# Two shared banks and a narrow layer norm in the windowed-attention layers, a later start for the weight loads, and a respaced state-space stage

## The reference, cut to what matters

```python
q, k = l2norm(q) * qs, l2norm(k) * ksc     # 16 heads of 64, then rotary tables on q and k
sim = jnp.einsum('bhwie,bhwje->bhwij', bq, bk2) * QK_SCALE
attn = jax.nn.softmax(jnp.where(mask, -jnp.finfo(sim.dtype).max, sim), -1)   # window 32
out = jnp.einsum('bhwij,bhwje->bhwie', attn, bv2)
...
def ffn_layer(x, g, bln, W1, b1, W2, b2):
    mu = x.mean(-1, keepdims=True)
    var = ((x - mu) ** 2).mean(-1, keepdims=True)
    xn = (x - mu) / jnp.sqrt(var + 1e-05) * g + bln
    hg = xn @ W1 + b1
    a, gate = jnp.split(hg, 2, -1)
    return a * jax.nn.gelu(gate, approximate=False) @ W2 + b2
for i in range(6):
    x = attn_layer(shift_tokens(x), ...) + x
    x = ffn_layer(shift_tokens(x), ...) + x
```

## Time and profile before

| | us |
|---|---|
| median of 3 runs | 6522.08 (6519.73 to 6525.92) |
| the profiled execution | 6522.74, its span 6520.8 |
| PE busy over the span | 5878.9 (90%) |
| DVE busy | 4384.8 (67%) |
| ACT busy | 3402.6 (52%) |
| POOL busy | 2289.2 (35%) |
| windowed attention, from its first projection (3236.6) to the end | 3284 |
| state-space stage, from its first measure (1791) to its last gather (2478) | about 690 |

### The profile page before, as it was taken

One profiled execution on the slowest core, in us unless ns is written; L12 is line 12 of the kernel. 1 busy time (PEld: TensorE's weight loads), 2 busy tenths in 40 slices (PEclk: granted clock), 3 DMA queues, 4 the chain that ended last, 5 costly groups with the idle time before them and its releaser, 6 DMA issues.

```text
span 6520.8 us, 129965 instructions
## 1 busy us (share of the span) xinstructions
PE 5878.9 (90%) x51681; PEld 3219.8 (49%) x51681; DVE 4384.8 (67%) x7178; ACT 3402.6 (52%) x5560; POOL 2289.2 (35%) x1597
## 2 busy tenths in 40 slices
PE   7999878999677778998689999999999999999998
PEld 3555554444422225765445555555555555555554
DVE  4656434454288894334678888888878788887885
ACT  3444324656144443444456656666666666665664
POOL 0111101222034441000055555555555555555553
PEclk9999978999688888998799999999999999999998
DMA  5555302333100000000011111111111111111110
GB/s 138 115 115 119 89 0 53 80 82 83 44 3 0 0 0 1 1 0 1 24 36 32 40 43 34 31 47 37 34 45 38 33 44 40 34 39 41 38 37 24
DMA packets 298945, 275.95 MB, mean 42 GB/s; under 512 B 40580, under 2 KB 289572, under 8 KB 298148
## 3 DMA queue, kind: packets, MB, share of 16 engines
q1 hardware_dynamic: 298372, 268.00, 17.7%
HBM read 30.88 MB, written 2.10 MB: 5 GB/s over the span
## 4 chain that ended last, share of the span: by engine, by line
PE 33%; issue 5%; DVE 5%; POOL 5%; ACT 2%; DMA 0%; POOLq 0%; DVEq 0%; SPq 0%; ACTq 0%
PE banks L2254 7%; PE banks L2289 6%; PE banks L2324 5%; PE banks L2309 4%; PE banks L2267 3%; PE banks L2341 3%; DVE local_probs L2559 2%; POOL local_rot L2653 2%; POOL local_ssum L2645 2%; PE banks L2363 2%; PE banks L2313 2%; PE banks L2274 1%; ACT local_probs L2455 1%; DVE local_gate L2584 1%; DVE local_sin L2540 1%
## 5 line engine op out<-in xcount | busy, mean ns | idle before, releaser
L2645 POOL TENSOR_TENSOR local_ssum<-local_sq 128x512 f32<-128x512 f32 x384 | 697.5, 1816 | 2145.1 <-ACT local_sq L2433 2144.6
L2653 POOL TENSOR_TENSOR local_rot<-local_rot,local_inv_all 128x512 f32<-128x512 f32 x768 | 964.6, 1288 | 94.1 <-DMA local_inv_all<-local_inv 93.6
L2254 PE MATMUL banks<-local_y,local_Wqkv 128*128 128x512 f32 x1536 | 823.0, 618 | 64.0 <-ACT local_sq L2433 61.2
L2559 DVE TENSOR_TENSOR local_probs<-banks,band 128x576 f32<-128x576 f32 x768 | 546.2, 753 | 185.4 <-PE banks L2289 180.1
L2455 ACT ACTIVATE local_probs<-local_probs,local_npeak 128x1152 f32<-128x1152 f32 x384 | 482.8, 1257 | 357.1 <-DVE local_probs L2559 357.1
L2539 DVE TENSOR_TENSOR local_rot<-banks,local_rotary_scaled 128x512 f32<-128x512 f32 x768 | 525.6, 684 | 191.1 <-PE banks L2254 185.6
L2433 ACT ACTIVATE local_sq<-banks 128x512 f32<-128x512 f32 x768 | 459.4, 598 | 253.6 <-DVE local_sin L2540 244.8
L2546 DVE TENSOR_TENSOR local_rot<-local_rot,local_sin 128x1024 f32<-128x1024 f32 x384 | 513.7, 1338 | 41.9 <-DVE local_sin L2540 2.3
L2449 ACT COPY local_v<-banks 128x512 f32<-128x512 f32 x384 | 224.9, 586 | 594.1 <-PE banks L2267 593.6
L2289 PEld LDWEIGHTS banks<-local_rot 32*128 32x128 f32 x12288 | 416.7, 186 | 225.0 <-issue 200.8
L2540 DVE TENSOR_TENSOR local_sin<-banks,local_rotary_scaled 128x512 f32<-128x512 f32 x768 | 522.4, 680 | 0.0
(11 more groups left out here) (400 smaller groups left out, 10561.4 us busy)
## 6 DMA issues: line engine op xcount, KB each, us to landing
local_inv_all<-local_inv SPq DMA_DIRECT2D x768, 128.0 KB, 2.7
favor_half_norm_all<-favor_half_norm SPq DMA_DIRECT2D x512, 128.0 KB, 3.0
cosine_inv_all<-cosine_inv SPq DMA_DIRECT2D x256, 128.0 KB, 2.6
favor_rden<-favor_inv SPq DMA_DIRECT2D x256, 64.0 KB, 2.1
cosine_rden<-cosine_inv_den SPq DMA_DIRECT2D x256, 64.0 KB, 2.1
local_Wqkv<-in_L_ffn_Wqkv_quads SPq DMA_DIRECT2D x36, 256.0 KB, 2.9
local_Wo<-in_L_ffn_Wo_quads SPq DMA_DIRECT2D x6, 512.0 KB, 4.1
experts_w_W<-in_L_ffn_W SPq DMA_DIRECT2D x1, 2048.0 KB
```

The lines of the kernel that those rows point to most:

```text
L2254: pe.matmul(seqs(banks[:, QK_BANK, :]), Wqkv[:, at:at + P], y_group(g), start=True, stop=True).then_inc(qk_projected, 1)
L2559: dve.tensor_tensor(probs[:, e % 3, r:r + 2, :], banks[:, S_BANK + r:S_BANK + r + 2, 0:SCORES], consts["band"].unsqueeze(1).broadcast_to([ ...
L2645: pool.tensor_tensor(ssum[:, n % 2, m, :], sq[:, 0, :], sq[:, 1, :], ALU.add).then_inc(square_summed, 1)
L2653: pool.tensor_tensor(a, a, twice(inv_all[:, n % 2, m, of_seq(s)]), ALU.mult).then_inc(united, 1)
```

## The change

- The start: only four constants, the weights of favor and x are loaded ahead of favor; the other five constants and the weights of router, cosine, int4, mamba and hgrn are issued by SP between favor's own transfers, in its steps 1 to 5.
- State space: measure, normalize, turn and copy of the next group stand four steps earlier (steps 12 to 15 of the group before); the output projection is cut in halves in steps 3 and 4, and the addition comes in step 5.
- Windowed attention, banks: P0 and P2 use bank 0, P1 and P3 bank 1, which they share with V0 and V1. The denominators go to bank 0, ahead of the values. `take_den` is cut in two: its Ln (`log_den`) stands ahead of the exponential of the probabilities, its Exp (`invert_den`) where the whole stood.
- PE's order: `score` of the even sequence stands ahead of `project_v(2i)` and `norm`. DVE masks ahead of the clamp, ACT squares ahead of the copy of v.
- The MLP's norm: means (step 4G+7) and variances (4G+8) are taken by 4 matmuls of 128 columns, each into 32 partitions, one per quarter of the tokens; ACT works on 128x128 instead of 128x512, and SP spreads each quarter back over 128 partitions by 4 transfers. POOL subtracts the mean (in place of the centering matrix and DVE's copy); `scale_mlp` stands behind `sum_squares(2i)`, no longer ahead of it.
- Ahead of the loop only group 0 is normed; groups 1 to 7 are measured, normed and turned in steps 0 to 7. The rotary tables are made in two halves, one of them at the end of the layer before.

```diff
+                    if i == LOADS:
+                        for tile, source in w["later_consts"]:
+                            sp.dma_start(tile, source).then_inc(w["consts_loaded"][0], 16)
+                    if 0 < i - LOADS <= len(w["later"]):
+                        w["later"][i - LOADS - 1].load(sp)
+                sp.wait_ge(*w["consts_loaded"])
...
-        0, 1, 2, 3, 5, 7, 8, 9, 10, 11, 12, 13, 14
-    GATE, WAY_OUT, ADD_OUT = 2, 3, 4
-    FIRST, LAST = -NS, N + ADD_OUT
+        -4, -3, -2, -1, 5, 7, 8, 9, 10, 11, 12, 13, 14
...
-    QK_BANK, V_BANK, S_BANK, O_BANK, X_BANK = 0, 1, 2, 6, 7
+    DEN_BANK, V_BANK, S_BANK, O_BANK, X_BANK = 0, 1, 2, 6, 7
+    qk_bank = lambda c: (DEN_BANK, V_BANK)[c % 2]
...
-                    if c:
-                        pe.wait_ge(squared, c)
+                    if half:
+                        pe.wait_ge(v_copied, c // 2 + 1)
+                    elif n >= 3:
+                        pe.wait_ge(den_logged, 2 * n - 5 + m)
+                    elif c:
+                        pe.wait_ge(squared, c - 1)
...
-                    if j >= 6:
-                        pe.wait_ge(den_logged, j - 5)
-                    elif j:
-                        pe.wait_ge(v_copied, j)
+                    if j:
+                        pe.wait_ge(squared, 2 * j)
...
+                    at_step = n + 2 + s
                     pe.wait_ge(exped, e + 1)
+                    if at_step < N:
+                        pe.wait_ge(squared, 4 * at_step + 3 - 2 * s)
+                    elif e:
+                        pe.wait_ge(den_logged, e)
+                    for lo, hi, tile in ((0, BAND, 0), (BAND, SCORES, 1)):
+                        for r in range(4):
+                            at = tile * P
+                            last = pe.matmul(banks[32 * r:32 * r + 32, DEN_BANK, at:at + hi - lo], consts["ones"][:, 0:32],
+                                             probs[:, e % 3, r, lo:hi], start=(tile == 0), stop=(tile == 1), skip_group_check=True)
+                    last.then_inc(den_summed, 1)
...
-                def center_mlp(G):
-                    take_x(centered, G + 1)
+                def mean(G):
+                    take_x(mean_taken, G + 1)
                     pe.wait_ge(added, 2 * G + 2)
-                    pe.matmul(seqs(banks[:, X_BANK, :]), center[:], y_group(G % GROUPS), start=True, stop=True).then_inc(centering, 1)
+                    for c in range(GT):
+                        at = c % ST * P
+                        last = pe.matmul(banks[32 * c:32 * c + 32, X_BANK, 0:P], consts["ones"][:, 0:32],
+                                         y[:, 2 * (G % GROUPS) + c // ST, at:at + P], start=True, stop=True)
+                    last.then_inc(y_summed, 1)
 
                 def variance(G):
                     take_x(var_logged, G + 1)
                     pe.wait_ge(mlp_squared, G + 1)
-                    pe.matmul(banks[:, X_BANK, :], consts["ones"], msq[:], start=True, stop=True).then_inc(var_summed, 1)
+                    for c in range(GT):
+                        last = pe.matmul(banks[32 * c:32 * c + 32, X_BANK, 0:P], consts["ones"][:, 0:32], msq[:, c * P:(c + 1) * P],
+                                         start=True, stop=True)
+                    last.then_inc(var_summed, 1)
...
                 for i in range(LAST + 1):
                     if i < N:
                         project(4 * i)
+                    if (e := within(2 * (i - 2))) is not None:
+                        score(e)
+                    if (G := mlp_at(i, 7)) is not None:
+                        mean(G)
+                    if i < N:
                         project_v(2 * i)
                     if 1 <= i <= N:
                         norm(i - 1)
-                    if (e := within(2 * (i - 2))) is not None:
-                        score(e)
...
-                def take_den(e):
-                    act.wait_ge(valued, e + 1)
+                def log_den(e):
+                    act.wait_ge(den_summed, e + 1)
                     if e >= 2:
                         act.wait_ge(normalized, e - 1)
-                    act.activation(rden[:, e % 2, :], banks[:, V_BANK, 0:SEQ], ACT.Ln, scale=UP).then_inc(den_logged, 1)
+                    act.activation(rden[:, e % 2, :], banks[:, DEN_BANK, 0:SEQ], ACT.Ln, scale=UP).then_inc(den_logged, 1)
+
+                def invert_den(e):
                     act.wait_ge(den_logged, e + 1)
...
+                def take_mean(G):
+                    act.wait_ge(y_summed, G + 1)
+                    if G:
+                        act.wait_ge(rstd_sent, 64 * G)
+                    act.activation(token_stat[:], banks[:, X_BANK, 0:P], ACT.Copy, scale=1.0 / D).then_inc(mean_taken, 1)
...
-                    act.activation(msq[:], banks[:, X_BANK, :], ACT.Ln, bias=eps[:], scale=1.0 / D).then_inc(var_logged, 1)
+                    act.wait_ge(mean_sent, 64 * (G + 1))
+                    act.activation(token_stat[:], banks[:, X_BANK, 0:P], ACT.Ln, bias=eps[:], scale=1.0 / D).then_inc(var_logged, 1)
                     act.wait_ge(var_logged, G + 1)
-                    act.activation(msq[:], msq[:], ACT.Exp, scale=-0.5).then_inc(rstd_done, 1)
+                    act.activation(token_stat[:], token_stat[:], ACT.Exp, scale=-0.5).then_inc(rstd_done, 1)
...
                 for i in range(LAST + 1):
+                    if (G := mlp_at(i, 7)) is not None:
+                        take_mean(G)
                     if i < N:
+                        square(4 * i)
                         copy_v(2 * i)
-                        square(4 * i)
                     if 1 <= i <= N:
                         invert_norm(i - 1)
+                    if (e := within(2 * (i - 3) + 1)) is not None:
+                        log_den(e)
                     if (e := within(2 * (i - 2))) is not None:
                         exp(e)
+                    if (G := mlp_at(i, 8)) is not None:
+                        square_mlp(G)
                     if i < N:
                         square(4 * i + 1)
                     if (e := within(2 * (i - 3) + 1)) is not None:
-                        take_den(e)
+                        invert_den(e)
                     if (G := mlp_at(i, 9)) is not None:
                         make_z(G)
                     if (G := mlp_at(i, 10)) is not None:
@@ -2503,39 +2563,43 @@
                     if i < N:
                         copy_v(2 * i + 1)
                         square(4 * i + 2)
+                    if 1 <= i < GROUPS:
+                        copy_x(act, i)
+                    if (G := mlp_at(i, 8)) is not None:
+                        root(G)
+                    if (G := mlp_at(i, 9)) is not None:
+                        take_gate(G, 0)
+                    if (e := within(2 * (i - 2))) is not None:
+                        log_den(e)
                     if (e := within(2 * (i - 2) + 1)) is not None:
                         exp(e)
-                    if (G := mlp_at(i, 8)) is not None:
-                        square_mlp(G)
-                    if (G := mlp_at(i, 9)) is not None:
-                        take_gate(G, 0)
+                    if i < GROUPS - 1:
+                        root_x(act, i + 1)
                     if i < N:
                         square(4 * i + 3)
                     if (e := within(2 * (i - 2))) is not None:
...
+                def center_mlp(G):
+                    pool.wait_ge(mean_sent, 64 * (G + 1))
+                    pool.tensor_tensor(seqs(yc[:]), y_group(G % GROUPS), seqs(yc[:]), ALU.subtract).then_inc(centered, 1)
...
                 for i in range(LAST + 1):
+                    if i < N:
+                        sum_squares(2 * i)
                     if (G := mlp_at(i, 9)) is not None:
                         scale_mlp(G)
-                    if i < N:
-                        sum_squares(2 * i)
                     if 1 <= i <= N:
                         for s in range(GB):
                             for m in range(2):
                                 unite(i - 1, s, m)
                     if i < N:
                         sum_squares(2 * i + 1)
+                    if (G := mlp_at(i, 7)) is not None:
+                        center_mlp(G)
...
+                def send_token_stat(into, sent):
+                    for c in range(GT):
+                        rows_c = token_stat[32 * c:32 * c + 32, :]
+                        source = bass.AP(rows_c.tensor, rows_c.offset, [rows_c.ap[0], [0, 4], rows_c.ap[-1]])
+                        sp.dma_start(into[:, c * P:(c + 1) * P], source).then_inc(sent, 16)
...
+                    if (G := mlp_at(i, 7)) is not None:
+                        send_mean(G)
+                    if (G := mlp_at(i, 8)) is not None:
+                        send_rstd(G)
                     if (G := turn_at(i)) is not None:
...
-                for n in consts:
+                for n in FAVOR_CONSTS:
```

208 lines of the change are left out of this document (121 added, 87 removed).

## The result

The changed kernel takes 6554.84 us (median of 5 runs, 6552.95 to 6566.34) against 6522.08 before: 1.0055 times the time before, 95% interval 1.0044 to 1.0066 (the quotient of the two medians is 1.0050). It is slower by 33 us, where 84 were forecast.

What follows compares the result with a forecast made beforehand. PE was taken to set the pace in windowed attention; +3.0 us per four-step group gave +137, then -10 - 22.6 + 5 - 19 - 6 made +84.4, forecast 6607 us. Range leaving out two in ten runs: 6525 to 6640.

Steps and rivals of the forecast that it cites:

- three new waits: Windowed attention, PE: P1 behind V's copy (0.9 in steps 4k and 4k+1), V1 behind a square (0.45), gate 0 behind z (1.77).
- once-only terms: Outside the repeated loop: tables -10, earlier loop start -22.6, early steps +5, start -19, state space -6 us.
- so P1's and V1's waits (1.0 and 0.45) stand in each: +5: Early windowed-attention steps, which have no MLP: both waits occur in each, +5 us, bounds -10 and +15.
- 41 to 48: Sign to look for: the first projection of windowed attention stands 41 to 48 us earlier than 3236.6.
- new wait 3: Step 4k+1: gate 0 waits for z, since the scaling now stands behind the sum of squares; PE idle 1.77 us.
- two old waits: Before, P2 waits 0.71 us for a square, the norm's sums 0.84 for DVE's last hide; both were to go.
- +127: Steps 8 to 190 of windowed attention: forecast to take 127 us more than before.
- Rival 1: Step 4k+1: z is early after all, so gate 0's wait vanishes; -81 us, 6526; chance 0.06.
- Rival 2: Windowed attention: the waits on bank 1 don't arise; -103 us, 6504, faster; chance 0.11.
- Rival 3: Contention of rotation and POOL, 1.02 us, falls into two more steps of each group; +93 us, 6700; chance 0.05.
- Rival 4: PE's clock falls in step 4k+1, its work taking twice as long; +500 us, 7110; chance 0.02.
- forecast's own range: Whole kernel: 6570 to 6640 us around the forecast of 6607; chance 0.66.
- milder but slower (6535 to 6570, a wait half covered): Whole kernel: slower than before but below the forecast's own range; chance 0.10.

Runs made afterwards that it cites:

- e2: Changed kernel with the copy of the first v ahead of the first square again on ScalarE: 6505.58 us, ratio 0.9983 to the kernel before.
- e1: Changed kernel with the MLP norm's scaling ahead of the first sum of squares again on GpSimd: 6522.96 us, ratio 1.0009 to the kernel before.
- e6: Changed kernel with x's four normalizing instructions per group moved on VectorE to behind the next step's clamp: 6551.25 us, ratio 1.0046 to the kernel before.
- e9: Kernel before with the addition ending the first rotation put behind the following normalization on VectorE: 6579.67 us in a single run, beside 6519.5.
- e8: Changed kernel with scaling and v-copy exchanged, old order of v, norm and score, means behind scores, x's normalization behind the clamp: 6442.12 us, ratio 0.9884.

## Why the prediction was right, and where it was not

**The side, and the cause: right.** PE sets the pace, its work stays the same (+0.1 us a group was forecast, -0.04 measured), and three new waits of a few tenths to a microsecond make the loss 46 times. All three stand where they were put, and P2 waits for nothing now. The profile names the copy of v for P1, in steps 4k and 4k+1, and z for gate 0; e2 and e1 take these waits away. V1's 0.26 is read off the distance: it starts at 3896.64, and the square that it needs ends at 3896.60.

**The once-only terms: right**, within 4 us each, but for the first eight steps. There the step "so P1's and V1's waits (1.0 and 0.45) stand in each: +5" left out that the four normalizing instructions would meet GpSimd's multiplications; +11.8 was measured in the profiled execution, and in that of e6 it is gone. The first projection stands 50.3 us earlier, a little more than the 41 to 48 that were to show it.

**The size: wrong.** The steps came out at 16.1, 16.6, 20.2 and 15.4 (medians) where 16.1, 17.5, 20.4 and 15.4 were forecast. The step that failed is in new wait 3: "the scaling 1.72 later (the sum takes 1.75)". The sum takes 1.28 there, and the scaling comes 1.22 later. After, POOL in that step (timeline):

```profile
3896.67 1.28 POOL L2712 TENSOR_TENSOR local_ssum<-local_sq 128x512 f32<-128x512 f32 x1 [6.09 <-ACT local_sq L2480]
3897.89 1.28 POOL L2728 TENSOR_TENSOR local_mlp_yc<-local_mlp_yc,local_mlp_sq 128x512 f32<-128x512 f32 x1
```

Half a microsecond, 45.75 times, is 23 us. I had seen that the addition and the sum get in each other's way, and read 1.75 as the undisturbed value and 2.27 as the disturbed one, because 1.75 was the commonest. The row for the right reading stood in the earlier trace rows: a scaling, which reads two tiles of 128x512 as the sum does, takes 1.28. And the timeline of DVE before has the addition across the start of that sum (4525.34 in the earlier trace rows):

```profile
4524.74 1.23 DVE L2546 TENSOR_TENSOR local_rot<-local_rot,local_sin 128x1024 f32<-128x1024 f32 x1
```

It ends at 4525.97, and the sum 1.12 us later. In the changed kernel the addition ends at 3896.54, ahead of the sum. The most frequent duration of an instruction needn't be its undisturbed one; e9 shows which is which.

The rest is mostly two distances on ScalarE, read from pairs of rows that did not measure the same thing. After, ACT in that step (timeline):

```profile
3894.58 0.38 ACT L2470 ACTIVATE local_rden<-banks 128x256 f32<-128x256 f32 x1 [0.33 <-PE banks L2334]
3894.86 1.25 ACT L2502 ACTIVATE local_probs<-local_probs,local_npeak 128x1152 f32<-128x1152 f32 x1
3896.01 0.59 ACT L2480 ACTIVATE local_sq<-banks 128x512 f32<-128x512 f32 x1
```

Ln to exponential is 0.28 us, not the 0.41 that stood between the Ln and the Exp that needs its result. Exponential to square is 1.15, not 1.20: before, that square also waited for VectorE's rotary product, which ended at 4524.63, 0.04 ahead of it. That shortens the chains to V1 and to z by 0.18, and P1's, whose other links came out 0.08 longer, by 0.10. From P1 to gate 0 are now 3900.12 - 3892.76 = 7.36 us, not 8.00. The waits of a group thus are 1.02 and 0.75 (P1), 0.26 (V1) and 1.15 (gate 0), 3.2 us together, where 4.1 were forecast; 0.9 less, times 45.75, is the 41 us between +127 and +85.5. The other 11 us between forecast and measured time come from the profiled execution's distance from its median.

One thing in the base was loose and did no harm: the two old waits, 0.71 and 0.84, leave 64.85 us of a group of 66.4, not 65.25. The 0.84 does not stand in every step 4k (in the group of the earlier trace rows PE stands still 0.9 us in all), and 65.2 is what PE's busy time gives, 2981.98 over 45.75.

**The rivals.** Rival 1 was 6526 for no wait at z at all. e1 makes it so and gave 6523, but that they agree is luck: rival 1 priced the wait at 81 us, and e1 gained 32, since the wait is shorter and part of the gain is given back. Rival 2, no waits on bank 1, did not come about; P1 waits in both steps. Rival 3 did not come about in the changed kernel, where P1 waits from group to group in steps 4k and 4k+1 alone, but in e1. Rival 4 was wrong for the loop, where the granted clock stays 1.00 in a step 4k+1 with 14.52 us busy of 16.53; in six of the first eight steps it is 0.82 to 0.89. Two of them (windows of after):

```profile
3228.77:3248.11 19.34, 15.05 (x188) 8.03 (x185) 17.49 (x31) 9.35 (x19) 10.31 (x9) 0.82 0.12 28
```
```profile
3282.60:3310.84 28.24, 22.29 (x204) 11.51 (x201) 21.24 (x37) 11.41 (x23) 12.56 (x10) 0.88 0.08 20
```

Both hold two long waits of PE each, of 1.8 to 2.6 us, and P1, which stands behind the second, takes 2.07 and 2.08 us. The Trainium skill, "TensorE: Matmul & The Clock Gate", section "Part 1: The HAM clock gate", has activity release a throttle that is there by default; these rows agree with that. The range, 6525 to 6640, holds the measured time only by its reach toward rival 1. The time lies outside the forecast's own range and in "milder but slower (6535 to 6570, a wait half covered)", which had a chance of 0.10. With the sum at 1.28 us the forecast would have been 6584.

## What to carry to other kernels

When two engines share a resource, take an instruction's undisturbed time from its shortest rows or from a like instruction, not from its median, and ask of each edit which pairs will meet then; a moved step can pay for itself and lose the gain to a meeting further on. A bank that is given a second user binds two chains together, and the order on the engine that empties it (copy ahead of square) decides whether that costs anything. Here it decided between a loss of 33 us and a gain. Where work of a tuned loop is removed, look at what it covered: the narrow norm was worth 10 us on one bank, and with its earlier start more than 140 in the order that had moved the chain.

## What the runs showed of the hardware

In these runs VectorE's addition of two SBUF tiles and GpSimd's tile operations ran one behind the other but for some 0.15 us: where one was blocked, it ended 1.08 to 1.14 us after the one that it met. The addition takes 1.23 us alone, and 2.25 or 2.36 where it starts beside a running multiplication (before, e1). The sum takes 1.27 us alone (e9), 1.75 where it starts with the addition half done (before), and 2.28 where that addition had itself been held up by a multiplication (e1). The profile puts the wait into the duration of the one that waits, not into idle time. The same holds for VectorE's scaling of an SBUF tile: four of 128x128 take 1.11 us alone (e6) and 3.99 beside the multiplications (after), and one of 128x4 that takes 0.17 elsewhere took 1.29 where a multiplication started with it (e8). The Trainium skill, "SBUF — State Buffer", section "Who interferes with whom", names both kinds (two SBUF inputs; a scaling or copy in the mode that uses both ports) and says that the second one fully blocks; all these rows agree, though none shows in which mode a scaling ran.

ScalarE started an instruction 0.28 us behind a 128x256 Ln that takes 0.38 where it doesn't need its result (after, 3894.58), and 0.41 behind it where it does (before, 4525.16 to 4525.57).
